# A two-layer graph convolution on one core: another order of ScalarE and VectorE, and six full fp32 slots instead of three

## The chip, the cores and the metric

The kernel runs on one core of a Trainium2 chip. A core has TensorE (PE), VectorE (DVE), ScalarE (ACT), GpSimd (POOL) and SyncE (SP), each with its own instruction stream, and 16 DMA engines that all of them share. The streams meet only at semaphores. The metric is the device time of one execution in microseconds, the median of several runs; lower is better.

## The reference

```python
h = jnp.maximum(_layernorm(x, axis=-1), 0.0)                 # x: 6250 x 512 fp32
# norm = -dinv[src] * dinv[dst], dinv = 1/sqrt(number of edges that leave a node)
def _cheb_conv(x, src, dst, norm, W0, W1, b):
    out = x @ W0
    tx1 = segment_sum(x[src] * norm[:, None], dst, num_segments=x.shape[0])
    return out + tx1 @ W1 + b
h1 = _cheb_conv(h, src, dst, norm, W1_0, W1_1, b1)
h1 = _layer_norm(h1, gamma, beta)
h1 = where(h1 >= 0, h1, 0.01 * h1)
out = x + _cheb_conv(h1, src, dst, norm, W2_0, W2_1, b2)
```

There are 100,000 edges, sorted by destination, and all weights are 512 x 512 in fp32.

## The kernel before

**Prologue.** All 6250 rows of x are loaded (SP). DVE and PE count the edges per source node in a histogram of 50 steps: DVE writes two one-hot tiles per step (line 626), PE multiplies them (line 854). Beside it ACT takes row sums and squares for the layer norm. Between histogram steps DVE does two small jobs on the edge list: `order()` (lines 571 to 580) after step 5, which checks that edges are sorted, and `bases()` (lines 588 to 620) after step 9, which finds the first node of each chunk from a few single edges that DMAs from ACT's queue bring (`edge_i`). `bases()` raises `base_ready`. Then come the four scale values of each node, written to `node_scales` in DRAM (SP, line 276), the normalised rows, written to `table[0]` in DRAM (SP, line 282), and the first weights.

**The layers.** Each of two layers goes through 53 chunks (`NC`). A chunk holds 15 slots of 128 edges and at most 128 destination nodes. Per chunk:

- GpSimd issues 15 indirect DMAs (line 346), one a slot, each bringing 128 rows of 2 KB from the table into `rows[u]`. There are two such sets of 15 tiles (u = 0, 1), so it can be up to two chunks ahead. It waits for the indices of its chunk (`idx_now`, copied by ACT at line 438 after ACT has handled the chunk two before) and, for each five slots, until PE has summed them two chunks before.
- A slot is summed by a matmul of a 128 x 128 one-hot tile (`hots`, DVE, line 717) with the 128 x 512 gathered rows into `tx_ps`. For the 12 slots in `SPLIT` the rows are split in two fp32r parts: ACT rounds them into PSUM (line 448) and into `high` (line 450), DVE subtracts to get `low` (line 724), and PE makes two fp32r matmuls (lines 927 and 929). For the other three slots PE makes one full fp32 matmul from the gathered rows (line 932), which stands in the trace as two records.
- When the 15 slots are in, a small matmul closes the chunk (`close`, line 894). ACT scales the sum (`take_tx`, line 458), PE transposes it (line 842), ACT copies the transpose out (`copy_txT`, line 464), and PE multiplies it with W1 (line 847).
- The chunk's own rows (SP, line 290) are transposed by PE, copied by ACT (`copy_own`, line 470) and multiplied with W0 (line 847).
- The epilogue of layer 0 is `conv_stats`, `norm1` and `finish1` on DVE (lines 743 to 769), with a square root (line 474) and `make_sloped` (line 481) on ACT. That of layer 1 is `finish2` (lines 776 and 780). SP stores the result (line 300).

**What sets the order.** It is written out by hand, one function per engine: `step` for PE, `act_step`, `dve_step` and `done` for SP. Each engine runs its list in order, so an instruction that waits holds up all behind it. While PE is in chunk i, PE also finishes chunk i-1 (its transposes after slot 4, its dense product after slot 7), and transposes chunk i's own rows after slot 9, for the dense product after slot 12. ACT and DVE put the epilogue of chunk i-1 between their slots of chunk i.

Layer 1 gathers from `table[1]`, so it starts only when layer 0 has been stored.

Of the kernel before, what the change touches and what calls it, by code (L numbers as in the profile page):

```python
# [33 lines left out]
def gnn_kernel(nc, x, src, dst, W10, W11, b1, gamma, beta, W20, W21, b2, out):  # L34
# [27 lines left out]
    SPLIT = (0, 1, 2, 3, 4, 6, 7, 8, 9, 10, 12, 14)  # L62
    NS = len(SPLIT)
    NLOW = 6
# [6 lines left out]
    assert HC % 2 == 0 and NT % 2 == 0 and NC % 2 == 1 and NS % NB == 0 and NS % NLOW == 0 and SLOTS % GW == 0  # L71
# [11 lines left out]
    with ctx:  # L83
# [23 lines left out]
        high = [sb(f"high{a}", [P, D], F32R)[:, :] for a in range(NS)]  # L107
        low = [sb(f"low{a}", [P, D], F32R)[:, :] for a in range(NLOW)]
# [17 lines left out]
        scal = sb("scal", [P, 2, 4])  # L126
# [20 lines left out]
        ownT, sloped = work[:, 0, :], work[:, 1, :]  # L147
# [54 lines left out]
        s_scal = [sem(f"scales_in{u}") for u in range(2)]  # L202
# [27 lines left out]
        def last_use(L, i, a, depth):  # L230

            if a >= depth:
                return (L * NC + i + 2) * SLOTS + SPLIT[a - depth] + 1
            return (L * NC + i + 1) * SLOTS + SPLIT[a - depth + NS] + 1

# [9 lines left out]
        def chunks_of(engine, step):  # L245

            step(0, 0, 0, True, True)
            with engine.Fori(0, NC // 2 - 1) as k:
                step(2 * k + 1, 1, k, False, True)
                step(2 * k + 2, 0, k + 1, False, True)  # L250
            step(NC - 2, 1, NC // 2 - 1, False, True)
            step(NC - 1, 0, NC // 2, False, False)

        @block.sync
        def _(sp):
# [31 lines left out]
            def load_chunk(L, i, u):  # L287

                first = sp.value_load(base_i[0:1, bass.ds(i, 1)], min_val=0, max_val=BASE_MAX)
                sp.dma_start(own[u], table[L][bass.ds(first, P), :]).then_inc(s_own[u], 16)  # L290
                sp.dma_start(scal[:, u, :], node_scales[bass.ds(first, P), :]).then_inc(s_scal[u], 16)
                if L == 1:
                    sp.dma_start(xin[u], x[bass.ds(first, P), :]).then_inc(s_xr[u], 16)

            def store_chunk(array, i, s):
                if isinstance(i, int) and i == NC - 1:
                    sp.dma_start(array[N - LAST:N, :], stage[P - LAST:P, :]).then_inc(s, 16)
                else:
                    first = sp.value_load(base_i[0:1, bass.ds(i, 1)], min_val=0, max_val=BASE_MAX)
                    sp.dma_start(array[bass.ds(first, P), :], stage).then_inc(s, 16)  # L300

            sp.wait_ge(s_base, 1)
            sp.wait_ge(s_scal_out, 16)
            sp.wait_ge(s_tab, 2 * 16 * NH)
            for L in range(2):
                if L == 1:
                    sp.wait_ge(s_tab1, 16 * (NC + 1))
                load_chunk(L, 0, 0)
                load_chunk(L, 1, 1)
                if L == 0:  # L310
                    for target, array in ((bias1, b1), (gam, gamma), (bet, beta), (bias2, b2)):
                        sp.dma_start(target, array.partition_broadcast(P)).then_inc(s_vec, 16)
                    for k, w in enumerate((W20, W21)):
# [3 lines left out]
                def done(i, u, load):  # L317
                    sp.wait_ge(s_ready, i + 3)
                    store_chunk(array, i, s)
                    if load:  # L320
                        load_chunk(L, i + 2, u)

                with sp.Fori(0, NC // 2 - 1) as k:
                    done(2 * k, 0, True)
                    done(2 * k + 1, 1, True)
                done(NC - 3, 0, True)
                done(NC - 2, 1, False)
                done(NC - 1, 0, False)
# [3 lines left out]
        def _(pool):  # L332
# [5 lines left out]
            def gather_chunk(L, i, u):  # L338
# [11 lines left out]
                with pool.If(bad["pool"] > 0):  # L350
# [13 lines left out]
                    pool.sem_inc(s_greset, 1)  # L364

# [12 lines left out]
        def _(act):  # L378
# [61 lines left out]
            def make_high(L, i, u, h, which):  # L440
                for c in which:
# [7 lines left out]
                    act.wait_ge(s_slot, last_use(L, i, a, NS))  # L449
                    nc.scalar.copy(high[a], rows[u][:, c, :]).then_inc(s_high, 1)  # L450

            def take_tx(L, i, u, h):
# [30 lines left out]
            def layer(L):  # L483
                def act_step(i, u, h, first, more):
# [5 lines left out]
                    if not first:  # L490
                        take_tx(L, i - 1, 1 - u, hp)
# [492 lines left out]
```

## Time and profile before

| | us |
|---|---|
| median of 3 runs (2385.42 to 2393.63) | 2389.45 |
| the profiled execution | 2386.95 |
| its span | 2385.1 |
| first gather of layer 0 issued at | 182.08 |
| first gather of layer 1 issued at | 1290.20 |

Times in the rows further down are microseconds from the start of the span. A row of a timeline gives start, duration, engine, line and operation, what is written and read, how many instructions, and in brackets how long the engine had been idle before it and what ended that. An instruction of SP's or POOL's queue that starts a DMA ends long before the data has landed. PEclk is TensorE's granted clock, where 1.00 is 2.4 GHz.

### The profile page before, as it was taken

To read this page: it belongs to the slowest core of one execution; us is meant where nothing else is said; L and a number is where in the kernel's file an instruction comes from. 1 tells how busy PE (TensorE), PEld (TensorE's weight loads), DVE (VectorE), ACT (ScalarE), POOL (GpSimd) and SP (SyncE) were. 2 spreads that over 40 slices of the span, in tenths; PEclk is the share of its full clock that TensorE was granted. 3 is DMA by queue.
4 is the path that set the end of the run, shared out by engine and by line. 5 is a ranking of instruction groups with operands and counts; after the bars stand their busy time and mean duration, and the time that the engine had idled before them with its cause. 6 is when DMAs were issued, how large, how long until landed. Compare 5 with 4: busy or idle time off the path is not lost.

```text
span 2385.1 us, 35572 instructions
## 1 busy us (share of the span) xinstructions
PE 1971.6 (83%) x6636; PEld 1099.5 (46%) x6636; DVE 1530.1 (64%) x3705; ACT 1667.3 (70%) x3312; POOL 1517.5 (64%) x1596
## 2 busy tenths in 40 slices
PE   3926888888888888888886888888888888888887
PEld 3923444444444444444443444444444444444444
DVE  4955777777677777767775566655555565555564
ACT  2846777777777777777775777777777777777775
POOL 0007776667766666676672777767777777777772
PEclk9999999999999999999998999999999999999999
DMA  9268777777777777777773788777777777777774
GB/s 219 24 223 291 233 234 216 217 219 218 218 219 218 215 219 219 217 220 215 217 221 107 236 249 249 237 231 235 233 232 230 228 231 235 231 233 233 233 233 123
DMA packets 200632, 519.36 MB, mean 218 GB/s; under 512 B 59529, under 2 KB 59654, under 8 KB 198108
## 3 DMA queue, kind: packets, MB, share of 16 engines
q0 software_dynamic: 127200, 416.91, 59.8%
q1 hardware_dynamic: 73038, 101.80, 13.6%
q10 hardware_dynamic: 370, 0.40, 0.1%
q8 instruction: 7, 0.11, 0.0%
q14 instruction: 17, 0.14, 0.0%
HBM read 478.36 MB, written 40.61 MB: 218 GB/s over the span
## 4 chain that ended last, share of the span: by engine, by line
PE 65%; DVE 14%; issue 8%; ACT 7%; DMA 3%; DVEq 1%; ACTq 1%; SPq 1%; POOL 0%; POOLq 0%
PE ps L847 30%; PE ps L932 11%; PE ps L929 10%; PE ps L927 7%; DVE low L724 6%; DVE hots L717 5%; PE ps L842 4%; ACT high L450 3%; ACT ps L448 2%; PE ps L854 2%; DMA edge_i<-in_dst_dram 2%; ACT arena L434 1%; DVE loc_now L712 1%; DMA arena<-table,idx_now 1%; SPq L282 1%
## 5 line engine op out<-in xcount | busy, mean ns | idle before, releaser
L346 POOL DMA_INDIRECT arena<-table,idx_now x1590 | 1517.0, 954 | 831.8 <-issue 672.7
L724 DVE TENSOR_TENSOR low<-arena,ps 128x512 fp32r<-128x512 f32 x1272 | 856.3, 680 | 338.3 <-ACT ps L448 337.1
L927 PE MATMUL ps<-high,hots 128*128 128x512 f32 x1272 | 707.5, 556 | 260.0 <-ACT high L450 259.6
L448 ACT CAST ps<-arena 128x512 fp32r<-128x512 f32 x1272 | 746.8, 587 | 91.3 <-DMA arena<-table,idx_now 49.0
L450 ACT CAST high<-arena 128x512 fp32r<-128x512 f32 x1272 | 784.6, 617 | 0.0
L929 PE MATMUL ps<-low,hots 128*128 128x512 f32 x1272 | 559.0, 439 | 106.2 <-DVE low L724 106.0
L927 PEld LDWEIGHTS ps<-high,hots 128*128 128x128 f32 x1272 | 245.0, 193 | 418.5 <-ACT high L450 239.2
L929 PEld LDWEIGHTS ps<-low,hots 128*128 128x128 f32 x1272 | 244.5, 192 | 388.7 <-DVE low L724 289.6
L717 DVE TENSOR_SCALAR hots<-iota_f,loc_now 128x128 fp32r<-128x128 f32 x1590 | 396.9, 304 | 3.7
L470 ACT COPY work<-ps 128x512 f32<-128x512 f32 x106 | 62.1, 585 | 409.5 <-PE ps L842 409.5
L932 PE MATMUL ps<-arena,hots 128*128 128x512 f32 x636 | 343.1, 623 | 0.0
L712 DVE COPY loc_now<-loc_all 128x15 f32 (+1 forms) x106 | 21.3, 201 | 292.8 <-PE ps L929 287.8
L847 PE MATMUL ps<-w,work 128*128 128x512 f32 x424 | 199.7, 615 | 0.0
L847 PE MATMUL ps<-w,arena 128*128 128x512 f32 x424 | 190.7, 592 | 0.7 <-ACT arena L464 0.7
L847 PE MATMUL ps<-arena 128*128 128x512 f32 x424 | 190.7, 592 | 0.7 <-ACT arena L464 0.7
L847 PE MATMUL ps<-arena,work 128*128 128x512 f32 x424 | 191.1, 594 | 0.0
L932 PEld LDWEIGHTS ps<-arena,hots 128*128 128x128 f32 x636 | 113.5, 194 | 51.8 <-issue 50.7
L842 PE MATMUL ps<-ident,arena 128*128 128x128 f32 x848 | 127.0, 272 | 1.8 <-ACT arena L458 1.8
L847 PEld LDWEIGHTS ps<-w,work 128*128 128x128 f32 x424 | 86.8, 205 | 85.1 <-issue 81.2
L854 PE MATMUL ps<-w 125*125 125x50 bf16 x800 | 91.3, 283 | 33.3 <-DVE w L626 32.6
L743 DVE SCALAR_TENSOR_TENSOR ps<-ps,scal,arena 128x512 f32<-128x512 f32 x53 | 40.2, 759 | 121.8 <-PE ps L847 121.8
L847 PEld LDWEIGHTS ps<-arena 128*128 128x128 f32 x424 | 80.3, 190 | 81.7 <-issue 76.1
(101 smaller groups left out, 1082.6 us busy)
## 6 DMA issues: line engine op xcount, KB each, us to landing
arena<-table SPq DMA_DIRECT2D x106, 256.0 KB
arena<-table,idx_now POOLq DMA_INDIRECT x1590, 3.7
arena<-in_x_dram SPq DMA_DIRECT2D x53, 256.0 KB, 4.1
table<-arena SPq DMA_DIRECT2D x52, 256.0 KB
out_dram<-arena SPq DMA_DIRECT2D x52, 256.0 KB
arena<-in_x_dram SPq DMA_DIRECT2D x10, 1120.0 KB
table<-arena SPq DMA_DIRECT2D x10, 1120.0 KB
w<-in_L_gnn_W_dram SPq DMA_DIRECT2D x2, 1024.0 KB, 11.0
```

Of the source, the lines that this page charges most:

```text
L346: nc.gpsimd.indirect_dma_start(out=rows[u][:, c, :], out_offset=None, in_=table[L][:, :], in_offset=bass.IndirectOffsetOnAxis(ap=idx_now[: ...
L448: nc.scalar.copy(high_ps[a % NB][:, :].bitcast(F32R), rows[u][:, c, :]).then_inc(s_hips, 1)
L450: nc.scalar.copy(high[a], rows[u][:, c, :]).then_inc(s_high, 1)
L470: nc.scalar.copy(ownT, tr_ps[:, :]).then_inc(s_ownT, 1)
L717: nc.vector.tensor_scalar(hot_of(u, c), iota_f[:, :], loc_now[:, u, c:c + 1], None, ALU.is_equal).then_inc(s_hot, 1)
L724: nc.vector.tensor_tensor(low[a % NLOW], rows[u][:, c, :], high_ps[a % NB][:, :], ALU.subtract).then_inc(s_low, 1)
L842: last = nc.tensor.transpose(to[:, k * P:(k + 1) * P], source[:, k * P:(k + 1) * P], ident[:, :])
L847: last = nc.tensor.matmul(to[:, :], source[:, k * P:(k + 1) * P], w[:, k, :], start=start and k == 0, stop=stop and k == KC - 1)
L854: last = nc.tensor.matmul(hist_ps[0:TR, 0:NT], rhot[:, u, c // 2, :, c % 2], qhot[:, u, c // 2, :, c % 2], start=False, stop=False)
L927: nc.tensor.matmul(tx_ps[u][:, :], hot, high[a], start=c == 0, stop=False)
L929: last = nc.tensor.matmul(tx_ps[u][:, :], hot, low[a % NLOW], start=False, stop=c == SLOTS - 1)
L932: last = nc.tensor.matmul(tx_ps[u][:, :], hot.bitcast(F32), rows[u][:, c, :], start=c == 0, stop=c == SLOTS - 1)
```

## The change

Six parts, all in one diff:

1. `SPLIT` has 9 slots instead of 12: slots 4, 8 and 12 join slots 5, 11 and 13 with the full fp32 matmul, so six slots are full. There are 9 `high` and 9 `low` buffers, one per split slot.
2. ACT's and DVE's steps have another order. ACT makes the first six splits of chunk i (slots 0, 1, 2, 3, 6, 7) before it takes chunk i-1's sum, and the epilogue that stands between them is that of chunk i-2.
3. PE transposes the own rows of chunk i+1 after slot 10 of chunk i; there are two `ownT` buffers. SP loads own rows four chunks ahead.
4. The four scale values of all chunks are kept in one tile. GpSimd loads them by a loop of 53 DMAs in the prologue, once; before, SP loaded them per chunk and layer (106 DMAs of 2 KB).
5. `order()` stands after histogram step 34 instead of 5, `bases()` after step 39 instead of 9.
6. The epilogues of the last two chunks stand at the end of a layer.

```diff
-    SPLIT = (0, 1, 2, 3, 4, 6, 7, 8, 9, 10, 12, 14)
+    SPLIT = (0, 1, 2, 3, 6, 7, 9, 10, 14)
     NS = len(SPLIT)
-    NLOW = 6
+    NBUF = 9
...
-        scal = sb("scal", [P, 2, 4])
+        scal = sb("scal", [P, NC * 4])
...
-        ownT, sloped = work[:, 0, :], work[:, 1, :]
+        ownT, sloped = [work[:, 0, :], work[:, 1, :]], work[:, 2, :]
...
+        def scale(i, n):
+
+            return scal[:, bass.ds(i * 4 + n, 1)]
...
+                def done(i, u):
+                    if at_most(i, NC - 5):
+                        sp.wait_ge(s_t2, L * NC + i + 3)
+                        load_own(L, i + 4, u)
                     sp.wait_ge(s_ready, i + 3)
                     store_chunk(array, i, s)
...
+            pool.wait_ge(s_base, 1)
+            pool.wait_ge(s_scal_out, 16)
+            with pool.Fori(0, NC) as i:
+                first = pool.value_load(base_i[0:1, bass.ds(i, 1)], min_val=0, max_val=BASE_MAX)
+                pool.dma_start(scal[:, bass.ds(i * 4, 4)],
+                               node_scales[bass.ds(first, P), :]).then_inc(s_scal, 16)
...
+                    highs(0, 2)
+                    copy_own(L, i, u)
+                    if L == 0 and at_least(i, 2):
+                        take_std(i - 2)
+                    highs(2, 4)
+                    if L == 0 and at_least(i, 2):
+                        make_sloped(i - 2, u)
+                    highs(4, 6)
+                    if at_least(i, 1):
...
+                        take_tx(L, i - 1, 1 - u)
+                    highs(6, 8)
+                    if at_least(i, 1):
                         copy_txT(L, i - 1)
...
+                    highs(8, NS)
...
-                if t == 5:
+                if t == 34:
                     order()
-                if t == 9:
+                if t == 39:
                     bases()
...
+                    lows(0, 2)
+                    if at_least(i, 2):
+                        if L == 0:
+                            epi = conv_stats(i - 2, u)
+                        else:
+                            finish2(i - 2, u, h - 1)
+                    lows(2, 3)
...
+                    slots(i, u, h, 8, 11)
+                    if at_most(i, NC - 2):
+                        transpose_own(L, i + 1, 1 - u, h + u)
+                    slots(i, u, h, 11, 14)
                     dense_own(L, i, u)
-                    slots(i, u, h, 13, SLOTS)
+                    slots(i, u, h, 14, SLOTS)
                     close(L, i, u)
```

TensorE, one chunk of the loop, from the dense product with W1 (line 847 before, 882 after) to the one with W0. Lines 927/929 (969/971 after) are a split slot's two matmuls, 932 (974) a full one, 842 (877) the transposes. Before:

```order
L847 MATMUL ps<-w,arena 128x512 x4
L923 REGISTER_ALU
L926 REGISTER_ALU
L927 MATMUL ps<-high,hots 128x512
L929 MATMUL ps<-low,hots 128x512
L923 REGISTER_ALU
L926 REGISTER_ALU
L927 MATMUL ps<-high,hots 128x512
L929 MATMUL ps<-low,hots 128x512
L842 MATMUL ps<-ident,arena 128x128 x4
```

The same place after:

```order
L882 MATMUL ps<-w,arena 128x512 x4
L965 REGISTER_ALU
L974 MATMUL ps<-arena,hots 128x512
L965 REGISTER_ALU
L968 REGISTER_ALU
L969 MATMUL ps<-high,hots 128x512
L971 MATMUL ps<-low,hots 128x512
L965 REGISTER_ALU
L968 REGISTER_ALU
L969 MATMUL ps<-high,hots 128x512
L971 MATMUL ps<-low,hots 128x512
L877 MATMUL ps<-ident,arena 128x128 x4
```

Slot 8 has become a full matmul, and the four transposes now stand behind slot 10 and belong to the next chunk.

ScalarE before, around the copy of the transposed own rows (line 470), which stands behind slot 9; line 474 is the square root of the chunk before:

```order
L448 CAST ps<-arena 128x512
L449 REGISTER_ALU
L450 CAST high<-arena 128x512
L470 COPY work<-ps 128x512
L447 REGISTER_ALU
L448 CAST ps<-arena 128x512
L449 REGISTER_ALU
L450 CAST high<-arena 128x512
L474 ACTIVATE std<-veps 128x1
```

After, the same copy (line 502) stands behind slot 1 of the chunk, with the square root (line 506) right behind it:

```order
L477 CAST ps<-arena 128x512
L478 REGISTER_ALU
L479 CAST high<-arena 128x512
L502 COPY work<-ps 128x512
L505 REGISTER_ALU
L506 ACTIVATE std<-veps 128x1
L477 CAST ps<-arena 128x512
```

GpSimd after, between the prologue and the first gather: a loop (line 390) of a register load (line 391) and a DMA (line 392), ahead of the load of the flag (line 396) that was its first work before:

```order
L390 UNCONDITIONAL_BRANCH
L390 ISA
L391 TENSOR_LOAD base_i
L391 ISA x2
L392 ISA
L392 DMA scal<-node_scales 128x4
L390 REGISTER_ALU
L390 COMPARE_AND_BRANCH
L396 TENSOR_LOAD flag_i
L396 ISA x2
```

The 53 rounds of this loop now stand in GpSimd's stream ahead of every gather.

## Rows read from the trace of the kernel before

**Rows 1.** The page: busy us of each engine, share of the span, instructions

```profile
PE 1971.6 (83%) x6636; PEld 1099.5 (46%) x6636; DVE 1530.1 (64%) x3705; ACT 1667.3 (70%) x3312; POOL 1517.5 (64%) x1596
```

**Rows 2.** Windows: stretch, length, busy of PE, PEld, DVE, ACT, POOL; PEclk, DMA share, GB/s

```profile
400.00:800.00 400.00, 349.35 (x1076) 188.69 (x1076) 288.50 (x707) 294.43 (x584) 280.10 (x294) 0.97 0.74 218
...
1300.00:1700.00 400.00, 341.09 (x1070) 183.32 (x1070) 235.53 (x592) 286.76 (x554) 292.55 (x307) 0.99 0.78 237
...
355.30:376.80 21.50, 18.87 (x56) 10.14 (x55) 14.79 (x36) 16.53 (x33) 15.49 (x17) 0.92 0.76 233
```

**Rows 3.** Timeline of TensorE: the matmul that closes a chunk; start, us, engine, line

```profile
213.53 0.23 PE L894 MATMUL ps<-zeros_b 128*128 128x128 bf16 x1
...
601.79 0.23 PE L894 MATMUL ps<-zeros_b 128*128 128x128 bf16 x1
621.61 0.23 PE L894 MATMUL ps<-zeros_b 128*128 128x128 bf16 x1
...
1274.74 0.23 PE L894 MATMUL ps<-zeros_b 128*128 128x128 bf16 x1
...
2374.42 0.23 PE L894 MATMUL ps<-zeros_b 128*128 128x128 bf16 x1
```

**Rows 4.** Timeline of GpSimd: first and last gather of layer 0, first of layer 1

```profile
182.08 1.10 POOL L346 DMA_INDIRECT arena<-table,idx_now  x1 [180.95 <-issue]
...
1249.98 0.95 POOL L346 DMA_INDIRECT arena<-table,idx_now  x1 [0.30 <-issue]
1290.20 1.06 POOL L346 DMA_INDIRECT arena<-table,idx_now  x1 [39.27 <-issue]
```

**Rows 5.** Gathers by line, 190 to 1249 and 1310 to 2350: busy, mean ns | idle

```profile
L346 POOL DMA_INDIRECT arena<-table,idx_now x788 | 750.1, 952 | 310.1 <-issue 224.8 <-ACT idx_now L438 59.1 <-PE ps L929 25.3
...
L346 POOL DMA_INDIRECT arena<-table,idx_now x779 | 744.8, 956 | 295.1 <-issue 221.3 <-PE ps L929 72.6 <-ACT idx_now L438 0.6
```

**Rows 6.** Chain that ended last, 2330 to 2345: start, us, what

```profile
2331.23 3.43 PE ps L847 x8
2334.66 0.86 PE ps L932 x2
...
2339.84 0.44 PE ps L842 x4
...
2341.83 0.23 PE ps L929
```

**Rows 7.** Waits in layer 0, 213 to 1272: in total, times, longest

```profile
ACT work L470 <- PE ps L842: 203.1, 52, 3.9
...
PE ps L927 <- ACT high L450: 89.1, 52, 1.8
```

**Rows 8.** Timeline of ScalarE: one split, and the first one of layer 1

```profile
607.97 0.59 ACT L448 CAST ps<-arena 128x512 fp32r<-128x512 f32 x1
...
608.49 0.62 ACT L450 CAST high<-arena 128x512 fp32r<-128x512 f32 x1
...
1294.94 0.59 ACT L448 CAST ps<-arena 128x512 fp32r<-128x512 f32 x1 [8.81 <-DMA arena<-table,idx_now]
```

**Rows 9.** Timeline of the prologue on VectorE, ScalarE and SP's queue

```profile
31.54 0.15 DVE L573 CAST viol<-nxt_i 125x1 f32<-125x1 int32 x1 [2.35 <-DMA nxt_i<-in_dst_dram]
...
53.06 0.18 DVE L588 CAST chunk_f<-edge_i 1x52 f32<-1x52 int32 x1 [12.27 <-DMA edge_i<-in_dst_dram]
...
120.85 0.72 ACT L410 ACTIVATE work<-arena,node_vec 125x512 bf16<-125x512 f32 x1 [7.46 <-DVE node_vec L636]
...
134.24 0.30 SPq L276 DMA_DIRECT2D node_scales<-scal_all  x1
```

**Rows 10.** GpSimd's one register load, line 367: ns min/median/max, start

```profile
L367 POOLq TENSOR_LOAD <-flag_i x1: 490/490/490, 55.6 to 55.6; - x1
L367 POOLq FUSED_REGOPS  x1: 182/182/182, 56.1 to 56.1; - x1
```

**Rows 11.** Chain at the end of layer 0: landing of the last store

```profile
1286.30 2.84 DMA table<-arena
```

More of the change, by code:

```diff
@@ L105, in gnn_kernel @@
         assert at_own + 8 <= NT
-        high = [sb(f"high{a}", [P, D], F32R)[:, :] for a in range(NS)]
-        low = [sb(f"low{a}", [P, D], F32R)[:, :] for a in range(NLOW)]
+        high = [sb(f"high{a}", [P, D], F32R)[:, :] for a in range(NBUF)]
+        low = [sb(f"low{a}", [P, D], F32R)[:, :] for a in range(NBUF)]
         hots = sb("hots", [P, 2 * SLOTS * P], F32R)
@@ L201, in gnn_kernel @@
         s_own = [sem(f"own_rows_in{u}") for u in range(2)]
-        s_scal = [sem(f"scales_in{u}") for u in range(2)]
+        s_scal = sem("scales_in")
         s_t2, s_ownT = sem("ownT_in_psum"), sem("ownT_ready")
@@ L245, in chunks_of, with at_least, at_most @@
         def chunks_of(engine, step):
[L247 to L252, printed above, removed]
+            step(0, 0, 0)
+            step(1, 1, 0)
+            with engine.Fori(0, NC // 2 - 2) as k:
+                step(2 * k + 2, 0, k + 1)
+                step(2 * k + 3, 1, k + 1)
+            for i in range(NC - 3, NC):
+                step(i, i % 2, i // 2)
+        def at_least(i, n):
+            return not isinstance(i, int) or i >= n
+        def at_most(i, n):
+            return not isinstance(i, int) or i <= n
         @block.sync
@@ L315, in _ @@
                 array, s, s_ready = (out, s_out, s_fin) if L else (table[1], s_tab1, s_hs1)
-                def done(i, u, load):
+                def done(i, u):
+                    if at_most(i, NC - 5):
+                        sp.wait_ge(s_t2, L * NC + i + 3)
+                        load_own(L, i + 4, u)
                     sp.wait_ge(s_ready, i + 3)
                     store_chunk(array, i, s)
[L320 to L328, printed above, removed]
+                    if L == 1 and at_most(i, NC - 3):
+                        load_residual(i + 2, u)
+                with sp.Fori(0, NC // 2 - 2) as k:
+                    done(2 * k, 0)
+                    done(2 * k + 1, 1)
+                for i in range(NC - 5, NC):
+                    done(i, i % 2)
             sp.wait_ge(s_out, 16 * (NC + 1))
@@ L782, in layer, with dve_step, lows @@
             def layer(L):
-                def dve_step(i, u, h, first, more):
-                    hp = h if u else h - 1
-                    def lows(*which):
-                        for c in which:
+                def dve_step(i, u, h):
+                    more = at_most(i, NC - 2)
+                    def lows(a0, a1):
+                        for c in SPLIT[a0:a1]:
                             make_low(L, i, u, c)
@@ L859, in _ @@
             nc.tensor.matmul(hist_ps[:, 0:NT], zeros_b[:, 0:P], zeros_b[:, 0:NT], start=True, stop=False)
-            for t in range(6):
+            for t in range(36):
                 histogram(t, t % 2)
@@ L864, in _ @@
                              stop=True).then_inc(s_violsum, 1)
-            for t in range(6, 12):
+            for t in range(36, 42):
                 histogram(t, t % 2)
```

182 lines of the change are left out of this document (89 added, 93 removed).

## The prediction, made before the changed kernel was run

> **What bounds the kernel now.** I read the page's busy shares first. No engine is at its limit on them: PE 83%, ACT 70%, DVE and POOL 64% [rows 1]. By stretches the two layers look alike, PE 0.87 and 0.85 of the time, DMA 0.74 to 0.78, clock 0.97 and 0.99 [rows 2]. So something is limited by order. The timeline of PE gives the period: closes of neighbouring chunks stand 19.8 us apart, 52 intervals of layer 0 average (1274.74 - 213.53)/52 = 20.4 us; some chunks have 21.5 us at a mean clock of 0.92 [rows 2, 3].
>
> Then each engine's own need per chunk. PE: the chain shows 0.23 us for a fp32r matmul, so 0.46 to 0.47 for a split slot, 0.86 for a full one (two records), 0.44 for four transposes, 3.43 for a dense product [rows 6]. Before: 12 x 0.47 + 3 x 0.86 + 2 x 0.44 + 2 x 3.43, with 0.1 for the close, is 16.1 us. The other 3.7 of 19.8 are waits: 89.1 us on `high` in 52 waits, up to 1.8 each, and many short ones on `low`; ACT in turn waits 203.1 us in 52 waits for the transpose of own rows before it can go on [rows 7]. ACT: a split starts 0.52 us after its first half began and takes as long again, 1.04 us; 12 x 1.04 + some 2.7 for the rest is 15.2. None of these reaches 20.
>
> POOL does. A gather is 0.952 us plus an idle gap of 0.30 (224.8 us over the some 740 gathers that wait for nothing), 1.26 us, in layer 1 the same from 0.956; fifteen are 18.9 us [rows 5]. In layer 0 it issues 795 gathers from 182.08 to 1250.9, 20.17 us a chunk [rows 4]; only 59.1 + 25.3 us of it are waits for ACT's indices and PE's slots [rows 5]. So POOL's floor lies 1.3 us a chunk below today's pace, and 2.8 above PE's need. That is what a better order can win, at most.
>
> **Slots and order, per chunk.** Three slots go from split to full. PE: + 3 x (0.86 - 0.47) = 1.2, so 17.3 us [rows 6]. ACT: - 3 x 1.04 = 3.1, so 12.1. DVE loses three subtractions. On TensorE this part alone is a loss; it pays only because ACT's chain was what PE waited for. The Trainium skill (FP8 and Floating Point Precision, TensorE Precision Notes) says the same against the change: true fp32 takes four passes through the array; the trace's 0.86 beside 0.23 agrees, and with four times 0.23 a full slot would be 0.92 and the sum 17.7 instead of 17.3.
>
> I walk the new order with these durations, zero at a close when nothing waits for data. ACT takes the sum by 0.9; PE does slots 0 to 4 (ready since the last chunk) by 2.7, transposes by 3.2, slots 5 to 7 by 5.0. ACT has made slots 9 and 10 by 3.0 and copied the transpose by 3.9, so the dense product (5.0 to 8.4) doesn't wait. Slots 8 to 10 end at 10.2, own transposes at 10.6, slots 11 to 13 at 13.2, dense at 16.7, close at 17.3. Meanwhile ACT: slot 14 and the indices by 5.2, next chunk's slots 0 and 1 by 7.3, wait for the own transposes until 10.8, then copy, root, slots 2, 3, `sloped`, slots 6, 7 by 16.7. It fits, with 0.5 us to spare. The waits on `high` and `low` that cost 3.7 us go, and what is late next is POOL's gather: the period becomes 18.9 us, if PE and ACT need no more than that when data arrive one slot per 1.26 us.
>
> So the same walk with zero at the landing of slot 0 of a chunk: ACT has slots 0 to 7 at 9.9 (slot 7 lands at 8.8), takes the old sum until 10.6, slots 9 and 10 by 13.5, copy by 14.2; PE transposes at 10.8, dense at 14.3 to 17.7, and closes the new chunk at about 26.5, 8.6 us after slot 14 landed (17.6) if it is the last one. From taking a sum to the next possible one are 17.2 us, under 18.9: a slack of 1.7 us, as much as a chunk loses at the lower clock [rows 2, 3]. POOL's two waits go: indices for chunk i+2 are copied when slot 14 of chunk i is done, a whole chunk before POOL asks. SP's longer list costs nothing: own rows are asked for some three chunks ahead, and what its new waits wait for comes before the finished result that it waits for today.
>
> Layers: after the last gather ends, 3.7 us until it can be used (first gather of layer 1: 1290.20 + 1.06 to 1294.94) [rows 4, 8], 8.6 to the close, then as before 1290.20 - 1274.74 = 15.5 to the first gather of layer 1, and 2385.1 - 2374.42 = 10.7 to the end [rows 3, 4]. Layer 0: 53 x 18.9 = 1001.7, + 12.3 + 15.5 = 1029.5, where it was 1108.1. Layer 1: 1001.7 + 12.3 + 10.7 = 1024.7, where it was 1094.9. Gain 149 us; 24 of it, 12 a layer, is that the last close comes 12 us after the last gather's end, not 24 (1274.74 - 1250.93).
>
> **Prologue.** DVE waited 12.27 us for `edge_i` and 2.35 for `nxt_i` [rows 9]. After step 34 both have long landed (53 us at the latest), so DVE's histogram ends 14.6 us sooner; the jobs themselves still cost DVE the same. ACT was waiting for DVE there (7.46 us) [rows 9], so nothing else is late first. Scales are sent at 134.24 - 14.6 = 119.6 [rows 9], and all that follows moves with them: the table would be ready for a gather at 182.08 - 14.6 = 167.5.
>
> But POOL now has 53 loads of scales in its stream first. They start when the scales have landed: 119.6 + 0.3 + 2.8 (a store's landing [rows 11]) = 122.7. No row shows a round of this loop. From below: if it hides, the first gather is at 167.5, a gain. Its parts: a register load 0.49 and register work 0.18, twice, plus branch and semaphore, about 1.05 [rows 10]; a DMA of 128 descriptors at a gather's pitch, 1.26 [rows 5]. If POOL's sequencer runs ahead while descriptors are written, a round is the larger, 1.3; if not, the sum, 2.3. I take 1.3, since a gather's 0.30 gap holds its own register work as well and these DMAs need no index. 53 x 1.3 = 68.9, first gather at 192.0. The early histogram is thus more than eaten: 24.5 us of loop on the path, net 10 us later than today. The 6784 packets of 16 bytes compete with the table's store, which has until 192 to land.
> The Trainium skill (DMA: Bandwidth & Descriptors, Anatomy of one DMA) puts about 2.0 us fixed on each DMA of this path; 53 in series would be 106 us, an estimate that would put the first gather at 229. The trace disagrees for gathers, which follow at 1.26 us, so the fixed part overlaps there.
>
> **Sum.** 192.0 + 1029.5 + 1024.7 = 2246.2 of span, + 1.85 outside it (2386.95 - 2385.1) = 2248. Before: 2386.95 in the profiled run, 2.5 below the median of 2389.45.
>
> **Rivals.**
> - Serial loop: a round takes 2.3 us. For it: nothing in the trace has a register load between POOL's DMAs. First gather at 244.9, so 2301.
> - The order doesn't reach POOL's floor: ACT's spare 0.5 us is used up by semaphores, or the lower clock (0.92 over a chunk [rows 2]) meets PE's higher need of 17.3, + 1.6 = 18.9. At 19.5 us a chunk, 106 x 0.6 = 64 more: 2312; with no gain in pace at all (20.2), 2385. Against it: PE's and ACT's sums are both below 17.4.
> - The loop hides altogether (rounds under 0.85 us): first gather at 167.5, 2224.
> - Slower than before: a round of the loop costs POOL 4 us or more. Its place is between 123 us and the first gather; it decides from (2389 - 2248 + 68.9)/53 = 3.96 us a round. At 5 us the first gather is at 388 and the time 2444. For it: direct DMAs with 16-byte rows are nowhere on POOL in the trace. Against: 128 descriptors with an index each need 1.26.
>
> **How the numbers follow.** Forecast 0.60 (2248, own range 2232 to 2272), serial loop 0.17, pace above the floor 0.13, hidden loop 0.05, slower 0.04, no change 0.01. No change means within 0.3%, 7 us, about what can be told. The range of 2216 to 2314 takes in the loop from hidden to serial and a pace of 19.5; its lower end lies 8 us under the hidden loop, for the 1.25 us pitch that most gathers have. Outside are the slower case and a pace above 19.5. Faster is 0.95.
>
> **What would show it.** POOL's rows: idle beside issue near zero, pitch 1.26, 15 in 18.9 us, closes of PE 18.9 us apart in both layers. ACT's long wait changes to one for gathers (DMA), and PE's waits on `high` move with it. The first gather between 185 and 200, `edge_i` wait gone, histogram's end near 117. It is wrong if closes stay at 19.5 or more, if POOL still waits for PE or indices, or if the loop ends after 200.

## The result, and the profile after

| | before | changed |
|---|---|---|
| median, us | 2391.26 (4 runs, 2385.42 to 2393.63) | 2269.15 (4 runs, 2267.3 to 2273.94) |
| span of the profiled run | 2385.1 | 2268.4 |
| first gather of layer 0 | 182.08 | 221.40 |
| layer 0, first gather to first gather | 1108.1 | 1024.9 |
| layer 1, first gather to the end | 1094.9 | 1022.1 |

The changed kernel takes 0.950 of the time of before, 95% interval 0.947 to 0.952. The forecast was 2248 us, range 2216 to 2314: right in its direction and range, 21 us too low. In the profiled run's own span the sum was 2246.2 and came out at 2268.4: the first gather 29.4 us later than forecast, layer 0 4.6 and layer 1 2.6 us shorter.

The page of the changed kernel, busy us and share of each engine, answers to [rows 1]:

```profile
PE 1972.2 (87%) x6636; PEld 1083.1 (48%) x6636; DVE 1358.1 (60%) x3387; ACT 1361.3 (60%) x2676; POOL 1543.1 (68%) x1650
```

ACT lost 306 us of work, DVE 172, PE's busy time is the same. The windows, with the columns of [rows 2]:

```profile
600.00:1000.00 400.00, 371.40 (x1170) 198.17 (x1169) 276.58 (x704) 263.57 (x512) 302.77 (x320) 1.00 0.79 236
...
1700.00:2200.00 500.00, 470.58 (x1464) 248.49 (x1463) 277.73 (x719) 307.13 (x584) 378.69 (x399) 1.00 0.81 250
```

POOL makes 320 gathers in 400 us, one per 1.25 us, where it made 294 [rows 2]; PE's clock in these windows is 1.00. The closes (PE's timeline, three neighbours, the last of layer 0 and the last of all) answer to [rows 3]:

```profile
911.09 0.23 PE L929 MATMUL ps<-zeros_b 128*128 128x128 bf16 x1
930.24 0.23 PE L929 MATMUL ps<-zeros_b 128*128 128x128 bf16 x1
949.08 0.23 PE L929 MATMUL ps<-zeros_b 128*128 128x128 bf16 x1
...
1231.18 0.23 PE L929 MATMUL ps<-zeros_b 128*128 128x128 bf16 x1
...
2257.72 0.23 PE L929 MATMUL ps<-zeros_b 128*128 128x128 bf16 x1
```

The first three stand 19.15 and 18.84 us apart. GpSimd's timeline, first and last gather of layer 0 and first of layer 1, answers to [rows 4]:

```profile
221.40 1.00 POOL L367 DMA_INDIRECT arena<-table,idx_now  x1 [1.28 <-issue]
...
1218.62 0.94 POOL L367 DMA_INDIRECT arena<-table,idx_now  x1 [0.30 <-issue]
1246.27 0.94 POOL L367 DMA_INDIRECT arena<-table,idx_now  x1 [26.71 <-issue]
```

(1219.56 - 221.40)/53 = 18.83 us a chunk. The gathers by line, 230 to 1200 and 1270 to 2200, answer to [rows 5]:

```profile
L367 POOL DMA_INDIRECT arena<-table,idx_now x773 | 735.2, 951 | 235.6 <-issue 215.5 <-PE ps L971 11.3 <-PE ps L974 6.1
...
L367 POOL DMA_INDIRECT arena<-table,idx_now x740 | 705.1, 953 | 225.6 <-issue 207.6 <-PE ps L971 7.3 <-PE ps L974 6.4
```

The 59.1 us of waiting for ACT's indices are gone, and nearly all idle time is the gap beside each issue: GpSimd sets the pace. (What is still put down to PE is never over 0.3 us each, the gap itself.) The waits of layer 0, 213 to 1232 (total, times, longest), answer to [rows 7]:

```profile
ACT ps L477 <- DMA arena<-table,idx_now: 315.8, 183, 84.3
...
PE ps L969 <- ACT high L479: 56.2, 9, 50.9
...
ACT work L502 <- PE ps L877: 2.2, 1, 2.2
```

ACT's 203.1 us in 52 waits for the own transposes have become one of 2.2 us. It now waits for gathers; two entries hold the start (84.3 and 50.9 us before the first slot is in). What is left of PE's 52 waits for `high` is 5.3 us in eight. One wait of ACT is there that the prediction's walk doesn't have: before the square root it waits for DVE's `veps`, 94.6 us in 51 waits. At GpSimd's pace it costs nothing in the changed kernel; it comes back below.

The scale loop. SP's queue sends the scales, and GpSimd's first two rounds and a later one:

```profile
119.87 0.30 SPq L288 DMA_DIRECT2D node_scales<-scal_all  x1
...
124.80 0.73 POOL L392 DMA_DIRECT2D scal<-node_scales  x1 [123.47 <-issue]
129.48 0.71 POOL L392 DMA_DIRECT2D scal<-node_scales  x1 [3.95 <-issue]
...
200.22 0.53 POOL L392 DMA_DIRECT2D scal<-node_scales  x1 [0.95 <-issue]
```

The scales go 14.4 us earlier than in [rows 9] (forecast 14.6). The loop starts at 122.4 (forecast 122.7), but a round is 1.5 us at best and up to 4.7 at the start, so that 53 take 97.7 us, not 68.9. The register load by itself, while the table is stored (120 to 165) and after (170 to 220); ns min/median/max:

```profile
L391 POOLq TENSOR_LOAD <-base_i x17: 293/1215/3418, 122.4 to 164.7; - x17
...
L391 POOLq TENSOR_LOAD <-base_i x33: 285/287/306, 170.7 to 218.4; - x33
```

And the same stretches by windows, DMA share in the last column but one, with a short one between them:

```profile
120.00:165.00 45.00, 0.00 (x0) 0.00 (x0) 21.36 (x59) 20.62 (x31) 9.33 (x16) 1.00 0.91 294
...
165.50:169.50 4.00, 0.00 (x0) 0.00 (x0) 0.00 (x0) 0.00 (x0) 1.60 (x3) 1.00 0.95 320
...
170.00:220.00 50.00, 1.09 (x4) 0.71 (x4) 0.00 (x0) 0.00 (x0) 18.06 (x34) 1.00 0.17 43
```

While the table is stored, with the DMA engines 0.91 busy, a load takes 1.2 us in the median; behind it 0.29. But the share alone isn't what makes it slow. In the short stretch the engines are 0.95 busy, and its loads (165 to 170 us) are as fast as the later ones:

```profile
L391 POOLq TENSOR_LOAD <-base_i x4: 285/289/293, 164.7 to 169.2; - x4
```

What has changed by then is what is moved. By the sizes of the packets, 1248 of 2275 in 120 to 165 are of 8 KB or more; in 165 to 170 there are three of 871: SP sent the last of the store by 160.0 and the weights after it. `edge_early`, `gather14` and `split12` below show the same: rounds of 1.5 us with the engines at 0.91 to 0.98, from 4 to 5 us after the store's last part was sent. Nor is it VectorE or ScalarE: both are idle from 145 to 165 us, and the loads there still take 1.1 us in the median, up to 1.8. So a load is slow beside the store of the table. What in the store slows it isn't shown.

### The profile page after: what moved, and what is told of

The parts are those of the page before. It is cut to its first block, busy times and chain, and to the rows that moved or that the text cites. A ratio compares the mean times of both kernels' runs of the same rounds, so it can differ in the third digit from the quotient of the medians.

```text
span 2268.4 us, 34019 instructions
## 1 busy us (share of the span) xinstructions
PE 1972.2 (87%) x6636; PEld 1083.1 (48%) x6636; DVE 1358.1 (60%) x3387; ACT 1361.3 (60%) x2676; POOL 1543.1 (68%) x1650
## 4 chain that ended last, share of the span: by engine, by line
PE 31%; POOL 27%; DMA 16%; issue 15%; ACT 6%; POOLq 3%; DVE 2%; ACTq 0%; DVEq 0%
POOL arena L367 27%; PE ps L882 16%; DMA arena<-table,idx_now 15%; PE ps L974 7%; ACT high L479 3%; PE ps L889 2%; PE ps L969 2%; PE ps L971 2%; POOLq L391 2%; ACT arena L492 2%; DVE w L661 1%; ACT ps L477 1%; PE ps L877 1%; DMA src_i<-in_src_dram 1%; ACT arena L486 1%
## 5 line engine op out<-in xcount | busy, mean ns | idle before, releaser
L759 DVE TENSOR_TENSOR low<-arena,ps 128x512 fp32r<-128x512 f32 x954 | 641.7, 683 | 799.0 <-ACT ps L477 741.7
L477 ACT CAST ps<-arena 128x512 fp32r<-128x512 f32 x954 | 561.1, 588 | 697.2 <-DMA arena<-table,idx_now 685.3
L974 PE MATMUL ps<-arena,hots 128*128 128x512 f32 x1272 | 622.8, 599 | 0.0
L479 ACT CAST high<-arena 128x512 fp32r<-128x512 f32 x954 | 586.1, 614 | 0.0
L969 PE MATMUL ps<-high,hots 128*128 128x512 f32 x954 | 518.3, 543 | 60.9 <-ACT high L479 60.9
L971 PE MATMUL ps<-low,hots 128*128 128x512 f32 x954 | 378.2, 396 | 0.0
L974 PEld LDWEIGHTS ps<-arena,hots 128*128 128x128 f32 x1272 | 227.5, 192 | 163.5 <-issue 150.0
L877 PEld LDWEIGHTS ps<-ident,arena 128*128 128x128 f32 x848 | 102.1, 141 | 215.1 <-issue 126.0
L882 PEld LDWEIGHTS ps<-w,arena 128*128 128x128 f32 x424 | 76.3, 189 | 162.3 <-ACT arena L492 86.1
L882 PEld LDWEIGHTS ps<-arena,work 128*128 128x128 f32 x424 | 80.6, 190 | 101.4 <-issue 99.5
```

The costliest lines, as they stand in the source:

```text
L477: nc.scalar.copy(high_ps[a % NB][:, :].bitcast(F32R), rows[u][:, c, :]).then_inc(s_hips, 1)
L479: nc.scalar.copy(high[a % NBUF], rows[u][:, c, :]).then_inc(s_high, 1)
L759: nc.vector.tensor_tensor(low[a % NBUF], rows[u][:, c, :], high_ps[a % NB][:, :], ALU.subtract).then_inc(s_low, 1)
L877: last = nc.tensor.transpose(to[:, k * P:(k + 1) * P], source[:, k * P:(k + 1) * P], ident[:, :])
L882: last = nc.tensor.matmul(to[:, :], source[:, k * P:(k + 1) * P], w[:, k, :], start=start and k == 0, stop=stop and k == KC - 1)
L969: nc.tensor.matmul(tx_ps[u][:, :], hot, high[a % NBUF], start=c == 0, stop=False)
```

## The experiments

Twelve kernels ran, in three series of four, each beside the kernel before on the same chip. The first series met a chip on which every kernel was disturbed: before took 3473 us there. Its four kernels are told by their repeats on another chip; their own numbers are in the last of these sections.

### The scale loop and the edge jobs

**The scale loop away from GpSimd** (`sp_scales`). SP loads a chunk's scales behind its own rows, into the same one tile:

```diff
+                if L == 0:
+                    if not isinstance(i, int) or i >= 2:
+                        sp.wait_ge(s_scal[u], 16 * h)
+                    sp.dma_start(scal[:, bass.ds(i * 4, 4)], node_scales[bass.ds(first, P), :]).then_inc(s_scal[u], 16)
...
-            with pool.Fori(0, NC) as i:
-                first = pool.value_load(base_i[0:1, bass.ds(i, 1)], min_val=0, max_val=BASE_MAX)
-                pool.dma_start(scal[:, bass.ds(i * 4, 4)],
-                               node_scales[bass.ds(first, P), :]).then_inc(s_scal, 16)
...
+                if L == 0:
+                    act.wait_ge(s_scal[u], 16 * (h + 1))
```

> The changed kernel with the scale values loaded from SP's queue chunk by chunk in layer 0 and no loop on GpSimd, again. Theory: the first gather comes at 167 to 168 us instead of 221.4 and all behind it is unchanged: 2216. Rival: something else ends near 220 as well and less than half of the 53 us comes back: 2243 or more.

Measured 2213.6 us (2209.49 to 2214.2), ratio to before 0.926 [0.925, 0.928]. GpSimd's timeline, first gathers of the two layers:

```profile
168.84 1.11 POOL L373 DMA_INDIRECT arena<-table,idx_now  x1 [167.70 <-issue]
...
1192.56 0.94 POOL L373 DMA_INDIRECT arena<-table,idx_now  x1 [26.87 <-issue]
```

The first gather is 52.6 us earlier, the time 55.5 us shorter; layer 0 is 1023.7. So the loop lies on the path with all it takes beyond the 167.5 that the forecast gave for a hidden one. This is the fastest of the kernels here that compute everything.

**The loop without its register load** (`loop_noload`).

```diff
-                first = pool.value_load(base_i[0:1, bass.ds(i, 1)], min_val=0, max_val=BASE_MAX)
...
-                               node_scales[bass.ds(first, P), :]).then_inc(s_scal, 16)
+                               node_scales[bass.ds(i * 117, P), :]).then_inc(s_scal, 16)
```

> The changed kernel with the register load taken out of the 53 rounds of the scale loop: the row is worked out from the round's number instead, so the scale values belong to other nodes; all else is as it was. Theory: the load is what a round waits for, beside the table's store above all; a round is then the 0.53 us of the DMA and a gather's gap of 0.30, the first gather is at 168 to 175 us and the time 2217 to 2224 us. Rival: the DMAs themselves are slow while the table is stored; rounds before 165 us stay at 1.3 to 4.7 us, later ones fall to 0.85, the first gather is at 195 to 205 us and the time 2243 to 2253 us.

Measured 2218.21 us (2217.18 to 2219.13), ratio 0.928 [0.926, 0.929]. GpSimd's timeline at the start and the end of the loop:

```profile
124.16 0.59 POOL L391 DMA_DIRECT2D scal<-node_scales  x1 [0.32 <-issue]
125.09 0.54 POOL L391 DMA_DIRECT2D scal<-node_scales  x1 [0.34 <-issue]
...
169.73 0.54 POOL L391 DMA_DIRECT2D scal<-node_scales  x1 [0.39 <-issue]
...
172.73 1.00 POOL L367 DMA_INDIRECT arena<-table,idx_now  x1 [1.53 <-issue]
```

A round is 0.93 us from first to last, with the DMA engines 0.96 busy all the while (122 to 172 us), first with the table's store and then with the weights. The rival is out: GpSimd's part in the DMAs was never slow, the load was. With its register work it costs 1.49 - 0.93 = 0.56 us a round behind the store, and 2.42 - 0.93 = 1.5 in the median beside it. The scale DMAs themselves landed later here, 6.0 us after issue in the median where in the changed kernel it is 1.9, and the rounds didn't wait for that.

**The edge jobs back behind steps 5 and 9** (`edge_early`).

```diff
-                if t == 34:
+                if t == 5:
                     order()
-                if t == 39:
+                if t == 9:
                     bases()
```

PE's two small matmuls for these jobs move along.

> The changed kernel with the two small edge jobs back behind histogram steps 5 and 9. Theory: VectorE waits again 12.3 and 2.35 us, the scales are sent some 14.4 us later, and everything behind moves with them: first gather at 236 us, 2283 to 2284 us. Rival: the scale loop gains as much when less of it lies beside the store of the table, and the time is 2269 to 2275 us.

Measured 2283.89 us (2280.45 to 2285.76), ratio 0.956 [0.954, 0.957]; VectorE waits again:

```profile
52.42 0.18 DVE L623 CAST chunk_f<-edge_i 1x52 f32<-1x52 int32 x1 [11.99 <-DMA edge_i<-in_dst_dram]
```

First gather at 235.31, 13.9 us later; 14.7 us more in all. The part is worth what its two waits were (the other, for `nxt_i`, is 2.59 us here).

### GpSimd as the floor

**One gather fewer** (`gather14`): slot 13's gather is left out.

```diff
+                    if c == 13:
+                        continue
...
+                            from_slot = 12 if c == 13 else c
```

> The changed kernel with one gather of 15 left out: slot 13 is summed from slot 12's rows, so the output leaves out slot 13's edges; TensorE's, ScalarE's and VectorE's work is the same. Theory: GpSimd's 15 gathers at 1.257 us set the period of 18.85; with 14 its floor is 17.6, TensorE's 17.3 us of work is next, so the period falls to 17.6 or a little more: 2269 - 106 x 1.2 = 2142 (up to 2160 if TensorE's own waits show). Rival: the period is TensorE's and ScalarE's chain as much as GpSimd's, and no more than a third of it comes: 2225 or more.

Measured 2134.77 us (2133.03 to 2136.35), ratio 0.894 [0.892, 0.895]. PE's closes in the middle of layer 0, the first and the last of four in a row:

```profile
602.29 0.23 PE L931 MATMUL ps<-zeros_b 128*128 128x128 bf16 x1
...
655.26 0.23 PE L931 MATMUL ps<-zeros_b 128*128 128x128 bf16 x1
```

52.97/3 = 17.66 us a chunk, 14 gathers at 1.26. 106 gathers fewer gave 2269.15 - 2134.77 = 134.4 us, 1.27 each, the whole price of their issue and 7 us more than was expected: the gathers are what bounds a layer in the changed kernel. PE, now 0.99 busy in its window (396.45 of 400), is next at once; the shortest chunks are 17.16 us, near the 17.3 that the forecast gave as PE's own need.

A gather left out takes its 256 KB off the DMA engines too, so this run alone can't tell their time from GpSimd's. The changed kernel's trace can. The second gather of layer 0 is issued when the DMA engines do almost nothing (0.15), and takes GpSimd no less than the later ones:

```profile
221.00:223.50 2.50, 0.00 (x0) 0.00 (x0) 0.00 (x0) 0.00 (x0) 1.79 (x2) 1.00 0.15 28
```

```profile
222.70 0.98 POOL L367 DMA_INDIRECT arena<-table,idx_now  x1 [0.30 <-issue]
```

Nor are the engines at their limit later: at the same pitch they move 236 GB/s in layer 0 and 250 in layer 1. So it is GpSimd's issue.

### Which of slots and order did it

**Six full slots in the old order** (`old_order9`): the kernel before with `SPLIT` of nine and `NLOW = 9`.

```diff
-    SPLIT = (0, 1, 2, 3, 4, 6, 7, 8, 9, 10, 12, 14)
+    SPLIT = (0, 1, 2, 3, 6, 7, 9, 10, 14)
-    NLOW = 6
+    NLOW = 9
```

> The kernel before with six full slots and 9 low buffers, all else as it was, again. Theory: its waits come from the order and stay, TensorE's work rises by 1.2 us: 19.6 to 20.4 us a chunk, 2350 to 2400. Rival: fewer splits alone reach GpSimd's floor of 18.85: 2250.

Measured 2371.17 us (2367.35 to 2373.91), ratio 0.993 [0.992, 0.995]; most closes are 20.2 us apart in both layers. ACT's wait and PE's, 213 to 1260:

```profile
ACT work L470 <- PE ps L843: 278.3, 52, 5.4
...
PE ps L928 <- ACT high L450: 89.1, 52, 1.8
```

ACT has less to do and waits longer, 278.3 us for 203.1, at the same place; PE's wait is the same to the tenth [rows 7]. The order was the limit, not ACT's load.

**Twelve split slots in the new order** (`split12`, nine buffers for the high and nine for the low parts, as in the changed kernel).

```diff
-    SPLIT = (0, 1, 2, 3, 6, 7, 9, 10, 14)
+    SPLIT = (0, 1, 2, 3, 4, 6, 7, 8, 9, 10, 12, 14)
```

> The changed kernel with 12 split slots (three full), so the new order alone; again, since on the chip of the first series every kernel, the one before too, ran with waits that no engine's work explains. Theory: GpSimd's 18.85 us for 15 gathers stays the period, TensorE's 16.1 and ScalarE's 15.2 us lie under it, so 2269 within 0.5%. Rival: ScalarE's three more splits, three of them behind the copy of the transpose, make it late: 19.3 us a chunk or more, 2317 or more. The first series speaks for the rival: there the new order alone was 18% slower than with six full slots.

Measured 2355.84 us (2354.95 to 2356.47), ratio 0.986 [0.985, 0.988]. By itself this reads as if the new order needed six full slots. But the loss stands in layer 0 alone. There the closes are 20.48 us apart, and from first gather to first gather it takes 1109.1 us (221.01 to 1330.08), 84.2 more than in the changed kernel. Layer 1 takes 1024.7, 2.6 more, and in its middle GpSimd makes 0.80 gathers per us as there:

```profile
1700.00:2200.00 500.00, 459.66 (x1452) 251.65 (x1451) 334.49 (x792) 378.98 (x741) 378.35 (x400) 0.97 0.82 251
```

ScalarE's waits in 600 to 1000 show what fills layer 0, and its timeline what it waited for:

```profile
ACT high L479 <- PE ps L971: 68.7, 57, 1.5
...
ACT std L506 <- DVE veps L786: 29.2, 19, 1.5
```

```profile
715.28 0.62 ACT L479 CAST high<-arena 128x512 fp32r<-128x512 f32 x1 [1.53 <-PE ps L971]
...
721.80 0.62 ACT L479 CAST high<-arena 128x512 fp32r<-128x512 f32 x1 [1.43 <-PE ps L971]
```

With nine buffers for twelve slots, the first three split slots of a chunk take the buffers of the last three of the chunk before (10, 12 and 14), and must wait until PE has summed those. With ACT's 299.6 us of work these two waits add up to 397.5 of the 400 us: in layer 0 ACT is busy or waits for a buffer or for `veps`, never for a gather. Layer 1 has no square root and no `sloped`. It waits for buffers too (192.1 us in 125 waits, 1400 to 2200), and still keeps GpSimd's pace in its middle. The next two runs change only the buffers.

**Twelve high buffers, six low** (`split12_h12`), as many in all as nine and nine:

```diff
-    NBUF = 9
+    NBUF = 12
+    NLOW = 6
```

These are also the split slots and the buffers of the kernel before, so what sets it apart from that kernel is the new order (parts 2, 3 and 6) and the moved scale loads and edge jobs.

> The new order with 12 split slots, but 12 buffers for the high parts and 6 for the low parts (as many in all as the 9 and 9). If the 9 and 9 buffers were what kept the new order with 12 split slots at 20.48 us a chunk (2355.8 us), ScalarE no longer waits for TensorE to free a high buffer, and closes come 18.9 to 19.3 us apart in both layers: 2270 to 2290 us. If it is the number of split slots itself (ScalarE has 15.2 us of work a chunk instead of 12.1, in one chain with the copies), the period stays at 19.7 or more and the time above 2320 us.

Measured 2258.94 us (2257.12 to 2262.32), ratio 0.945 [0.944, 0.947], 11 us below what was expected of it. The window of the middle of layer 0:

```profile
600.00:1000.00 400.00, 366.43 (x1173) 198.11 (x1171) 325.20 (x767) 326.61 (x640) 302.51 (x321) 1.00 0.79 238
```

Again 0.80 gathers per us, with ACT at 0.82 of the time where the changed kernel has 0.66. First gathers at 217.87 and 1237.71, end at 2255.4: layers of 1019.8 and 1017.7 us, both faster than the changed kernel's, by 5.1 and 4.4 us, and 88.3 and 77.2 less than before's. That is the worth of the new order without the six full slots. (The scale loads that have left SP's queue are worth nothing in it: with them back in layer 0, `sp_scales` has 1023.7 us beside 1024.9.) The low parts went from nine buffers down to six, so it was the high ones that were short. In the medians the kernel is 10 us faster than the changed one, each measured beside before, on different chips; the intervals of the two ratios, 0.9437 to 0.9469 and 0.9472 to 0.952, just don't meet. Some 3.5 us of that is the scale loop, which ended earlier in this profile and is the same code. So twelve split slots are possible in the new order and at least as good as nine. By these numbers the same buffers with the scales on SP would give about 2258.9 - 55.5 = 2203 us, an estimate; it wasn't run.

**Ten and ten** (`split12_buf10`):

```diff
-    NBUF = 9
+    NBUF = 10
```

> The same with 10 buffers for the high and 10 for the low parts. Buffers as the limit: ScalarE's waits for reuse shrink with each buffer, so the time lies between 2290 and 2340 us, below the 2355.8 us of nine. Number of splits as the limit: 2350 to 2360 us, unchanged.

Measured 2607.36 us (2605.25 to 2608.68), ratio 1.091 [1.089, 1.092]. Both theories had this wrong: one more buffer of each kind costs 251 us, 172.7 of it in layer 0 and 79.3 in layer 1 by the profiled spans (1281.8 and 1104.0 us), and makes the kernel 9% slower than before. The waits of 600 to 1000 show where:

```profile
DVE low L759 <- PE ps L971: 123.5, 33, 4.1
ACT high L479 <- PE ps L971: 114.2, 33, 3.7
...
POOL arena L367 <- ACT idx_now L467: 86.6, 16, 5.5
```

Buffers are numbered anew in each chunk (`a % NBUF`). With nine it is the third split slot that takes the buffer of slot 14, the last that PE sums; with ten it is the second. ACT can then be one slot ahead of the chunk's end, not two, waits up to 3.7 us there, and the indices that GpSimd needs, behind it in ACT's stream, come late. That is how the rows read; no run changed this wait alone. PE's clock is 0.85 in that window, against 0.91 with nine and 1.00 with twelve. PE's timeline shows what stands before its low stretches:

```profile
702.96 0.50 PE L969 MATMUL ps<-high,hots 128*128 128x512 f32 x1 [2.52 <-ACT high L479]
...
707.75 1.11 PE L877 MATMUL ps<-ident,arena 128*128 128x128 f32 x4 [0.24 <-ACT arena L486]
708.65 1.92 PE L974 MATMUL ps<-arena,hots 128*128 128x512 f32 x2
```

After an idle time of 2.52 us and three shorter ones the transposes take 1.11 us and the full slot 1.92, with a granted clock of 0.50 from 706 to 708 us, where with twelve buffers, after shorter idle times, they take 0.66 (below) and 1.02, with a clock of 1.00. So waits cost a second time through the clock. How much of the 251 us is clock and how much the wait was not taken apart.

### The disturbed series

| | us | ratio to before there | repeat on another chip |
|---|---|---|---|
| before | 3473.08 | | 2388.78 |
| `sp_scales` | 2604.81 | 0.750 [0.744, 0.756] | 0.926 |
| `edge_early` (one of its four executions took 7130.43) | 2674.36 | 0.770 [0.764, 0.777] | 0.956 |
| `split12` | 3148.14 | 0.907 [0.902, 0.913] | 0.986 |
| `old_order9` | 3548.47 | 1.022 [1.016, 1.028] | 0.993 |

What was expected, in the order of the table:

> The changed kernel, but the scale values are again loaded chunk by chunk from SP's queue (in layer 0 only, 53 DMAs of 2 KB behind the own rows), and GpSimd has no loop in the prologue. Theory: the loop of 53 rounds, 122.4 to 220.1 us, is all that holds up the first gather, which the table would allow at some 167 to 168 us. First gather near 168 instead of 221.4, all behind it unchanged: 2269 - 53 = 2216. Rival: another thing that ends near 220 (the weights for layer 0, or own rows) would hold layer 0 up as well, so that less than half of the 53 us comes back: 2243 or more.

> The changed kernel with order() after histogram step 5 and bases() after step 9, as before. Theory: VectorE waits again 12.3 + 2.3 us for the single edges, scales go out 14.6 us later (134.3 instead of 119.9), and GpSimd's loop starts and ends that much later: 2269 + 14.6 = 2284. Rival: the loop's slow first rounds (2.3 us instead of 1.49) come from the table's store beside it; both move together, so the loss stays 14.6. Second rival: the early place was hidden behind something and the time is the same within 0.3%.

> The changed kernel with 12 split slots as before (three full), so the new order alone. Theory: in the new order TensorE needs 16.1 us a chunk and ScalarE 15.2, both under GpSimd's 18.85 us for 15 gathers, so the period stays at 18.85 and the time at 2269 within 0.5%; the six full slots bring nothing by themselves. Rival: ScalarE's three more splits (3.1 us a chunk, idle 0.36 of the time in the changed kernel) take its slack, since it gets slots 9, 10, 12 and 14 late: period 19.3 or more, 2269 + 106 x 0.45 = 2317 or more.

> The kernel before with the new set of 9 split slots (six full) and 9 low buffers, all else as it was: the six full slots alone. Theory: the waits on high and low come from the order (copy of own transposes right after slot 9, subtractions between one-hots after the close), so most of them stay, PE's work rises from 16.1 to 17.3 us a chunk and the period stays between 19.6 and 20.4: 2350 to 2400. Rival: ScalarE's shorter list alone reaches GpSimd's floor of 18.85: 2389 - 106 x 1.3 = 2250.

None of the times expected was met, and the sizes say nothing on the question. The longest wait of `sp_scales` there, and its window in layer 0:

```profile
ACT work L503 <- remote: 921.8, 94, 21.2
```

```profile
230.00:1000.00 770.00, 660.62 (x1859) 335.86 (x1857) 437.43 (x1103) 403.19 (x805) 480.78 (x507) 0.91 0.67 196
```

Waits of up to 21 us whose releaser the trace can't name, a lower clock and 507 gathers where the repeat has 615 in the same window: where they come from stays open. All that can be said is that the new order suffered less from it than the old.

## Why the prediction was right, and where it was not

**GpSimd as the floor: right.** A chunk takes 18.83 us (forecast 18.9) in layer 0, idle time beside the gap is gone, and `gather14` moves the time by the price of its gathers. That it is GpSimd's time and not the DMA engines' the first gathers show. The new order removed ACT's long wait and PE's for `high`, as walked, and ACT waits for gathers instead. The walk priced ACT's wait for DVE's `veps` at nothing; it is 1.9 us a chunk in layer 0 (94.6 in 51), which the pace of the gathers hides. Which piece of parts 2, 3 and 6 does how much was not taken apart: every kernel in the new order has them all.

**Drain and hand-over: right.** From the last gather's end to the last close 11.6 us (12.3 forecast), to layer 1's first gather another 15.1 (15.5).

**The edge jobs: right**, 14.4 us in the trace and 14.7 in the time.

**The scale loop: on the path as forecast, but its two halves in series and not side by side, and this is the 21 us.** By the prediction's own sign ("if the loop ends after 200") this part was wrong: it ended at 220.1. The step that failed is "I take 1.3, since a gather's 0.30 gap holds its own register work as well". The loop was put at 68.9 us and took 97.7, a mean round of 97.7/53 = 1.84 us. The mistake was in what the two bounds were made of. The DMA was priced too high (1.26 from a gather; it is 0.93 with gap), and the register load was thought to run ahead, when it stands in series with the DMAs (without it, in `loop_noload`, the first gather came 48.7 us sooner, as 53 rounds of 0.93 for 1.84 make) and, above all, is slow beside the table's store. The price itself was in the trace: beside [rows 10], one load of 490 ns at 55.6 us, SP's queue has 106 of 269 ns in the median (line 289, from 181 us on). What was not there is a load beside the table's store, the stretch to which the loop was moved. Rounds of 1.49 us throughout would have been 79 us, 10 more than forecast; the other 19 are the slow ones. Of the two ends the serial 2.3 was slightly nearer to the truth than the 1.3. With 1.84 the sum is 192.0 + 53 x 0.54 = 220.6 for the first gather (measured 221.4) and 2276.6 in all; the layers gave 7 back, so the small error of the total is in part luck.

The Trainium skill (DMA: Bandwidth & Descriptors, Anatomy of one DMA), with some 2.0 us fixed per DMA, gave 229 as an estimate, which is nearer than the forecast's 192, but for the wrong reason: in the changed kernel these DMAs land 1.9 us (median) after issue, which agrees with the Trainium skill as a latency, yet without the load they follow each other at 0.93 us, though they landed 6.0 us after issue there. It isn't paid in series.

**The six full slots: the argument was wrong.** "It pays only because ACT's chain was what PE waited for" holds neither in the old order (`old_order9`: 0.7%, with ACT's wait grown) nor in the new (`split12_h12`: twelve split slots are no slower, the layers 9.5 us shorter). What ACT's chain lacked was a place in the order, not time. That full slots are a loss on TensorE alone does stand. The changed kernel needs its nine split slots only because it has nine buffers for the high parts, and only in layer 0, where ACT has the epilogue's waits as well; the forecast took the buffers for a detail of part 1 and priced them at nothing. It was luck that this did no harm: with nine split slots and nine buffers each slot has its own.

**Where the time came from**, in the profiled spans (116.7 us less): 83.2 and 72.8 from the layers, 14.4 from the edge jobs, less 53.7 for the loop (221.40 against 182.08 - 14.4).

## What to carry to other kernels

When waits go by reordering, ask next which buffer each early instruction inherits, and from which late one: the number of buffers matters less than whose last use is waited for, and one buffer more can be worse. Look at each layer by itself: the same shortage cost 84 us in one and 3 in the other. Before work is moved off an engine that is "busy 70%", check that its wait is not one of order: here the same engine at 82% was fast enough. And price a register load by what is moved in the stretch it will stand in, not by the DMA engines' share: beside the store of a table it was four times as dear. A load that another queue can make where it has time may cost nothing, as SP's did here.

## What the runs showed of the hardware

- A register load from a tile on GpSimd's queue took 1.2 us in the median, up to 3.4, beside the store of the table with the DMA engines at 0.91; 0.29 right behind it with the engines still at 0.95, and 0.29 with them at 0.17.
- A plain DMA of 128 rows of 16 bytes took GpSimd 0.53 us in the median, up to 0.79 in the first rounds, and 0.93 a round with loop and gap while the DMA engines were 0.96 busy. An indirect one of 128 rows of 2 KB took 0.95 + 0.30, and 0.98 + 0.30 with the engines at 0.15.
- One more buffer of each kind made a kernel 11% slower (2607.36 for 2355.84 us), by waits and by the clock that fell behind them.
- The granted clock fell to the lower of its levels, 1.2 GHz, after short idle times of TensorE: at the same place of a chunk idle times of 0.23, 0.85, 0.28 and 0.41 us (nine buffers) stood before transposes of 1.11 us (granted clock 0.50 from 707 to 708 us), and idle times of 0.85, 0.29 and 0.42 (twelve) before transposes of 0.66 (1.00 from 701 to 703). Rows for both:

PE's timeline with nine buffers for twelve split slots:

```profile
703.04 0.49 PE L969 MATMUL ps<-high,hots 128*128 128x512 f32 x1 [0.23 <-ACT high L479]
...
704.88 0.50 PE L969 MATMUL ps<-high,hots 128*128 128x512 f32 x1 [0.85 <-ACT high L479]
705.66 0.50 PE L971 MATMUL ps<-low,hots 128*128 128x512 f32 x1 [0.28 <-DVE low L759]
706.58 1.11 PE L877 MATMUL ps<-ident,arena 128*128 128x128 f32 x4 [0.41 <-ACT arena L486]
```

and with twelve:

```profile
699.72 0.49 PE L970 MATMUL ps<-high,hots 128*128 128x512 f32 x1 [0.85 <-ACT high L480]
700.50 0.50 PE L972 MATMUL ps<-low,hots 128*128 128x512 f32 x1 [0.29 <-DVE low L760]
701.42 0.66 PE L878 MATMUL ps<-ident,arena 128*128 128x128 f32 x4 [0.42 <-ACT arena L487]
```

One wait more, of 0.23 us, is what these rows show to differ just ahead. Whether that or what came earlier decides wasn't tested.
